# Third layer: VectorE forms the second experts' sums of all batches, and ScalarE fills two buffers of the attentions

## The reference, cut to what matters

```python
x = x + layer_norm(experts_of_layer_1(layernorm(x)), gamma, beta)   # the sum in question
x = x + mlstm(layernorm(x), ctx, ctx, gates, out_gain)
x = x + sigmoid(r) * (square(relu(k)) @ W_v.T)                       # channel mixing over time steps
```

## Time and profile before

| | |
|---|---|
| median of 3 runs | 1398.53 us (1395.99 to 1401.62) |
| the profiled execution's own time | 1400.19 us |
| its span, first to last instruction | 1398.1 us |
| TensorE's mean granted clock in it | 0.973 of full speed |
| busy: TensorE, VectorE, ScalarE, GpSimd | 90%, 61%, 34%, 33% |
| the third layer's loop (window 0 to the last output) | 782.98 to 958.6 us of the span |
| start of the second and of the fourth attention | 323.3 and 960.8 us |

### The profile page before, as it was taken

How to read it: one execution, slowest core, us unless ns; L and a number is a source line. 1 busy time by engine, 2 the same in 40 slices (tenths; PEclk the granted TensorE clock), 3 DMA queues, 4 the chain that set the end, 5 groups by cost and what they waited for, 6 DMA issues and landing times. The chain is left out here.

```text
span 1398.1 us, 31670 instructions
## 1 busy us (share of the span) xinstructions
PE 1258.8 (90%) x9966; PEld 1008.9 (72%) x9966; DVE 852.8 (61%) x2809; ACT 474.4 (34%) x1119; POOL 463.3 (33%) x435
## 2 busy tenths in 40 slices
PE   5899799997899998899999888897899998899995
PEld 4677589995566665789887666686566665799995
DVE  5788544445577876444575476755567776465563
ACT  3555211112556554011111244453556654111110
POOL 1145612223134334423122256533134343222231
PEclk9999899999999999999999998999999999999998
DMA  9101234422111401464655100000001011646523
GB/s 312 66 17 36 93 103 139 136 65 80 34 36 40 164 33 51 140 205 149 198 174 168 28 8 1 1 1 24 8 17 48 32 40 53 207 100 150 145 46 87
DMA packets 87556, 120.07 MB, mean 86 GB/s; under 512 B 11248, under 2 KB 64752, under 8 KB 87152
## 3 DMA queue, kind: packets, MB, share of 16 engines
q1 hardware_dynamic: 48656, 55.20, 12.9%
q10 hardware_dynamic: 25632, 34.85, 7.6%
q0 software_dynamic: 13152, 28.54, 7.2%
HBM read 82.53 MB, written 38.13 MB: 86 GB/s over the span
## 5 line engine op out<-in xcount | busy, mean ns | idle before, releaser
L1349 PEld LDWEIGHTS bank<-f_xT,f_up 128*128 128x128 f32 x2144 | 253.6, 192 | 13.3 <-issue 6.3
L1349 PE MATMUL bank<-f_xT,f_up 128*128 128x128 f32 x2144 | 258.5, 276 | 2.4 <-DVE f_xT L1225 2.1
L415 DVE TENSOR_REDUCE mha_nmax<-bank 128x2 f32<-128x512 f32 x256 | 170.0, 686 | 117.2 <-PE bank L558 93.5
L1358 PE MATMUL bank<-f_down,f_hT 128*128 128x256 f32 x832 | 199.5, 382 | 4.4 <-DVE f_hT L1266 2.3
L308 ACT ACTIVATE l_took<-bank 128x512 f32<-128x512 f32 x256 | 139.0, 598 | 129.8 <-PE bank L566 129.8
L558 PE MATMUL bank<-l_took,mha_q 32*128 32x256 f32 x1024 | 146.3, 402 | 34.5 <-DVE mha_nmax L415 22.1
L1358 PEld LDWEIGHTS bank<-f_down,f_hT 128*128 128x128 f32 x832 | 149.4, 190 | 24.8 <-DVE f_hT L1266 4.6
L1114 POOL DMA_INDIRECT yout<-f_y,f_to x66 | 81.1, 1229 | 244.9 <-DVE f_y L1302 107.0
L558 PEld LDWEIGHTS bank<-l_took,mha_q 32*128 32x128 f32 x1024 | 90.1, 186 | 74.5 <-DVE mha_nmax L415 45.0
L566 PE MATMUL bank<-l_took 32*128 32x256 f32 x1024 | 142.8, 400 | 0.7 <-ACT l_took L308 0.7
L1165 ACT ACTIVATE f_hT<-bank,f_b 128x128 f32<-128x128 f32 x148 | 46.4, 364 | 276.0 <-PE bank L1349 276.0
(11 more groups left out here) (293 smaller groups left out, 2284.9 us busy)
## 6 DMA issues: line engine op xcount, KB each, us to landing
l_took<-rows SPq DMA_DIRECT2D x91, 132.0 KB
f_up<-in_W ACTq DMA_DIRECT2D x23, 512.0 KB, 4.8
f_down<-in_W ACTq DMA_DIRECT2D x18, 512.0 KB, 5.4
l_took<-rows SPq DMA_DIRECT2D x21, 264.0 KB
f_up<-in_W SPq DMA_DIRECT2D x9, 512.0 KB, 7.3
ring<-yout SPq DMA_DIRECT2D x8, 512.0 KB, 3.9
mha_ctxT<-in_ctxT SPq DMA_DIRECT2D x16, 256.0 KB, 2.9
f_down<-in_W SPq DMA_DIRECT2D x6, 512.0 KB, 7.5
```

Of the source, the lines that this page charges most:

```text
L415: vector.tensor_reduce(nmax[:, p, :, at], ps_s[n % 2][:, :].rearrange("p (k s) -> p k s", s=S), AX.X, ALU.min).then_inc(max_ready, 1)
L1349: ins = pe.matmul(into, up[q][i][:, c, m * P:(m + 1) * P], xT[:, c, :], start=c == 0, stop=c == DC - 1)
L1358: ins = pe.matmul(ps_y[:, 0:D], hT[:, m, :], down[q][:, m, :], start=m == 0, stop=m == HC - 1)
```

## The change

It has three parts. In the third layer's loop the sums of batches 3 to 7 are formed as those of batches 0 to 2: `z_centre` takes the place of `z_normalize`, and `z_in` stands last in the window; `z_normalize` and GpSimd's `z_add` are gone, and with them two semaphores. In VectorE's order of a window, `mix(.., 1)` moves ahead of `mean_and_var`, and `outputs` moves ahead of `scale`. In both attentions, ScalarE fills `nmax` and `vaug` with two activations after its first small products, and GpSimd fills nothing.

```diff
             else:
-                    pool.memset(nmax[:, :, :, :], 0.0).then_inc(zeros_ready, 1)
-                    pool.memset(vaug[:, :, :, :, :], 1.0).then_inc(ones_ready, 1)
...
         act.wait_ge(nbq_ready, 1)
+        first = lambda n: G.consts[:, 0:1].to_broadcast([P, n])
+        act.activation(nmax[:, :, :, :].rearrange("p a k q -> p (a k q)"), first(2 * TPB * P), ACT.Identity,
+                       scale=0.0).then_inc(zeros_ready, 1)
+        act.activation(vaug[:, :, :, :, :].rearrange("p r i h v -> p (r i h v)"), first(2 * TPB * HEADS * VW), ACT.Identity,
+                       bias=1.0, scale=0.0).then_inc(ones_ready, 1)
...
-            def z_add(b):
-                pool.wait_ge(z_scaled, b + 1 - RING)
-                z_ = fused[:, b % RING, :, :]
-                pool.tensor_tensor(z_, z_, gamma[:, :].unsqueeze(1).to_broadcast([P, TPB, D]), ALU.mult).then_inc(z_gained, 1)
-                pool.wait_ge(z_gained, b + 1 - RING)
-                x = X[:, pair(b), :]
-                pool.tensor_tensor(x, x, z_, ALU.add).then_inc(z_added, 1)
...
                     z_root_of(w_ + 3)
-                    z_add(w_ + 3)
...
-            def z_normalize(b):
-                vector.wait_ge(z_root, b + 1)
-                for i in range(TPB):
-                    z_ = fused[:, b % RING, i, :]
-                    ins = vector.tensor_scalar(z_, z_, z_moments[:, b, i, 0:1], z_rstd[:, b, i:i + 1], ALU.subtract, ALU.mult)
-                ins.then_inc(z_scaled, 1)
...
             def z_centre(b):
-                    z_ = fused[:, b, i, :]
+                    z_ = fused[:, b % RING, i, :]
...
             def z_in(b):
-                    ins = vector.scalar_tensor_tensor(out=x, in0=fused[:, b, i, :], scalar=z_rstd[:, b, i:i + 1], in1=x,
+                    ins = vector.scalar_tensor_tensor(out=x, in0=fused[:, b % RING, i, :], scalar=z_rstd[:, b, i:i + 1], in1=x,
...
                     weigh(w_, 3)
+                if w_ >= LAG:
+                    mix(w_ - LAG, 1, k_mixed)
                 if w_ + 2 < B:
                     mean_and_var(w_ + 2)
-                if w_ >= LAG:
-                    mix(w_ - LAG, 1, k_mixed)
...
                 if w_ + 3 < B:
-                    z_normalize(w_ + 3)
+                    z_centre(w_ + 3)
...
                     maxima(w_ + 1)
+                if w_ >= LAG:
+                    outputs(w_ - LAG)
                 if now:
                     scale(w_)
...
                     tops(w_ + 1)
-                if w_ >= LAG:
-                    outputs(w_ - LAG)
+                if w_ + 3 < B:
+                    z_in(w_ + 3)
```

More of the change, by code:

```diff
@@ L264, in gpsimd_program @@
                     normalize(pool, b)
-                else:
-                    pool.memset(nmax[:, :, :, :], 0.0).then_inc(zeros_ready, 1)
-                    pool.memset(vaug[:, :, :, :, :], 1.0).then_inc(ones_ready, 1)
                 pool.wait_ge(xn_ready, b + 1)
@@ L1869, in l2 @@
         fused_in, gamma_in = [sem(f"fused{r}_in") for r in range(RING)], sem("gamma_in")
-        z_ready, z_root, z_scaled, z_gained, z_added = sem("z_ready"), sem("z_root"), sem("z_scaled"), sem("z_gained"), sem("z_added")
+        z_ready, z_root, z_added = sem("z_ready"), sem("z_root"), sem("z_added")
         w, mu = sb("w", [P, 3, DC, D]), sb("mu", [P, 2, DC])
```

## The result

| | before | after |
|---|---|---|
| median | 1398.05 us (17 runs, 1393.81 to 1403.71) | **1387.65 us** (17 runs, 1380.62 to 1394.95) |
| ratio, 95% interval | | 0.9922 [0.9904, 0.994] |
| profiled execution: time, span | 1400.19, 1398.1 us | 1390.65, 1388.9 us |
| its mean granted clock | 0.973 | 0.967 |

The forecast was 1387.2. It came out, but not along its own steps: the third layer's loop gained more than forecast in windows 0 to 3, and lost in windows 4 and 5 what no term of the sum had in it.

What follows compares the result with a forecast made beforehand. The loop was taken as bound by VectorE's order, with GpSimd's steps in it. Third layer -8.8 and fills -2.6 summed to -11.4 us, so a median of 1387.2 us; range 1380 to 1393.5.

Steps and rivals of the forecast that it cites:

- The wait for the root and `z_normalize`: Windows 1 to 4, VectorE: `z_normalize` goes with its wait for GpSimd's root of the sum, 0.72 + 0.73 = 1.45 us less.
- the holds of the two small operations: Windows 1 to 4: without GpSimd's `z_add`, VectorE's L2201 and L2230 fall to 0.17, 2.11 us less a window.
- rival (a): Third layer's loop: `z_centre` is held whole, 1.28 us in each of five windows, +6.4 us, 1393.6; chance 0.07.
- the wait for fT: Windows 1 to 4: the mix for k, now right behind the last `weigh`, waits for ScalarE's copy, 0.17 us more.
- the paragraph on the rule: By the Trainium skill's SBUF exclusion rule, `z_centre` would be held for one of L1954's two instructions; total -5.0 us.
- the root's collision with `gains`: Windows 1 to 4: GpSimd's root of the sum, pushed later, may hold `gains` for 0 to 0.72 us; 0.3 taken.
- After rows 2 and 3 such operations do not run together, whoever is first: `z_in`, between `scale` and `f_mean_and_var`, meets GpSimd's L1969 and L1973: whole 0.88 us added, lower bound 0.
- the clock: Windows 1 to 4: TensorE, denser, regains half of 1.18 us, -0.6 a window, bounds 0 and -1.18; a gap remains.
- rival (d): Windows 1 to 4: the clock comes back fully and `z_in` hides half, 4 x -1.0 more, 1383; chance 0.05.
- that on `outputs`: VectorE's order: `outputs` (0.68 us) moves into the 1.13 wait for the mLSTM's root ahead of `scale`; counted as 0.
- Rival (c): Windows 1 to 7: `outputs` becomes the wait, TensorE falls to its lower level from `project_r`; 27 us lost, near 1414; chance 0.04.
- three signs: Wrong would be: `z_centre` beyond 1.3 us, L2268 (`outputs`) waiting for TensorE in windows 1 to 4, or granted clock under 0.87.

## Why the prediction came out, and where it was wrong

**Where it was right.** The wait for the root and `z_normalize`, 1.45, and the holds of the two small operations, 2.11, went as forecast; `z_centre`, which rival (a) had held for 1.28 more, was not held; the wait for fT is 0.17. The fills give 2.5 by the two starts (1.56 and 0.98), for 2.6 forecast. One reading was wrong without harm: the paragraph on the rule names the mix for k, but the row under L1954 that is 0.23 longer is the mix for r, as the sum has it. Window 6 is 0.38 longer for 0.45.

**Terms that were mis-sized, nearly all to the careful side.** In window 2: `z_centre` 0.87 for 1.11, and the mix for r 0.87 for 1.11 beside 0.18 more in `log_forget`; the root's collision with `gains` 0 for 0.3; `z_in` 0.30 for 0.88 (`scale` starts at 836.12, the next window at 839.91: 3.79, before 3.49). The step "After rows 2 and 3 such operations do not run together, whoever is first" missed who loses: VectorE's operation is stretched to 1.89, inside time in which it waited, and GpSimd's two steps, which X needs, grow only from 1.27 to 1.51 and 1.33. And the clock: the last `weigh` ends 4.85 us after the window's start (825.11 + 1.02 - 821.28), before 6.02, so 1.17 came back and not half of it. In the order of the sum, with the wait for fT: -1.45 - 2.11 + 0.87 - 0.24 + 0.18 + 0.17 + 0.30 - 1.17 = -3.45; the window became 3.32 shorter. Where the clock held, then, the loop did what rival (d) had, some 2.7 us a window and 1383 in all; the versions without the move of `outputs` came to 1380.17 to 1383.37.

**The step that failed** is that on `outputs`: that it "moves into the wait of 1.13 for the root" and "this is 0 here". On VectorE's path that is nearly so in window 2: `outputs` waits 0.34 us for TensorE, which the prediction had ahead in windows 1 to 4, but `scale` starts right behind the root. But TensorE's `qk` waits for `outputs` of the window before, as the section on the kernel has it, and with that wait gone its idle time went into the one ahead of `turn_z`. For the clock I had bounds of 0 and -1.18, so no loss, though the paragraph on the clock said that a gap remains there. The lower level cost 5.55 us in window 4 (24.18 for the 18.63 of window 2) and 4.78 in window 5 (22.13, against 17.35 with the gap filled). Rival (c) had this mechanism, with the fall in `project_r` and not already in `values`, and in seven windows of a run where two or three fell; its outcome, a slower kernel, did not come. Of the three signs that I named for a wrong prediction, two appeared: `outputs` waits for TensorE (0.34 to 1.04 us, windows 2 to 4), and the clock is under 0.87 (0.72, window 4).

**How it adds up.** In the profiled executions windows 0 to 3 gained 12.5 us (7.5 forecast), windows 4 and 5 lost 6.75 (a gain of 1.7 forecast). All runs together say the same: without the move of `outputs` the rest gains 16.4 us where the sum had 11.4, so the sum was 5.0 too careful, and the move, which it had at 0, costs 5.4. These two errors cancel. That 1387.65 came so near to 1387.2 is luck, and not a sign that the sum was right.

**What stays open.** Why the clock falls behind the gap in some windows and not in others: in window 2 of the change the gap was the longest, 1.13, and nothing fell, and with `outputs` back one window fell behind 0.53. So the length of the gap alone does not tell whether a fall follows. The medians of the versions without the move of `outputs` (1380.17 to 1383.37) can't be ranked by these runs; the loop is shortest with neither move (18.33 to 18.38 in windows 2 to 4, 18.53 with the mix's move).

## What to carry to other kernels

When a wait of a nearly saturated TensorE is removed, ask where its idle time goes: if nothing else is faster it gathers at the next wait, and one gap of 0.7 to 1.1 us can cost more through the clock, as here, than two of about 0.5. A product of no use in that gap was the test here, and that or the old wait left in place the cure. And for two engines that collide on SBUF, ask which of them loses and whether that one had slack, before counting an operation's whole length.

## What the runs showed of the hardware

- TensorE's granted clock was 0.52, nearly all at the lower level, for some 14 and 10.6 us, beginning within 1 us behind idle times of 0.88 and 0.70 us. Behind 1.13 us in window 2 of the same run it stayed at 1.00, and it stayed there in windows 1 to 5 where two products of 128 by 256 filled the place.
- VectorE's two-input operations on 128 by 256 were stretched from 0.88 to 1.89 and 2.45 us for two beside GpSimd's two-input operations, while those took 1.27 to 1.51 us each (1.27 before); beside a GpSimd operation with one input it was the other way round (`z_centre` 0.87; GpSimd's normalization 3.08, for 2.45 without `z_centre` in the same place).
- GpSimd's fills, which read nothing, had stretched two VectorE operations with one tensor as input to 2.5 us; without them the two take 0.74.
